# The order of weight and input loads on SyncE's DMA queue in a two-layer attention kernel

## The reference, cut to what matters

```python
def layer(x, emb, mask, ...):                 # H = 16 heads in layer 0, 8 in layer 1
    xn = layernorm(x) * norm_scale + norm_bias
    q, k, v = xn @ Wq + bq, xn @ Wk + bk, xn @ Wv + bv
    # masked rows are left out of the softmax of k over the rows, and of v
    q = softmax(q, within a head)
    k = softmax(k, over the 128 rows)
    attn = einsum('bhsd,bhse->bhde', k, v)
    y = einsum('bhtd,bhde->bhte', q, attn)
    scale, shift = split(silu(emb) @ film_W + film_b)
    h = layernorm(y) * film_norm_scale + film_norm_bias
    h = h * (1 + scale) + shift
    return x + silu(h) @ Wo + bo
out = layer1(layer0(x))
```

## Time and profile before

| | us |
|---|---|
| median of 3 runs | 878.68 |
| the profiled execution | 877.97 |
| its span, first to last instruction | 876.2 |
| TensorE busy | 843.5 (96%) |
| VectorE busy | 679.9 (78%) |
| ScalarE busy | 607.6 (69%) |
| GpSimd busy | 549.5 (63%) |

### The profile page before, as it was taken

How to read it: one execution, slowest core, us unless ns; L and a number is a source line. 1 busy time by engine, 2 the same in 40 slices (tenths; PEclk the granted TensorE clock), 3 DMA queues, 4 the chain that set the end, 5 groups by cost and what they waited for, 6 DMA issues and landing times.

```text
span 876.2 us, 19904 instructions
## 1 busy us (share of the span) xinstructions
PE 843.5 (96%) x6581; PEld 715.2 (82%) x6581; DVE 679.9 (78%) x1352; ACT 607.6 (69%) x1441; POOL 549.5 (63%) x741
## 2 busy tenths in 40 slices
PE   4989999999999999999978999999999999999997
PEld 4768888888888888888867888888888888888885
DVE  5987777778778778877977887787788788777765
ACT  5566777676777677677775866776776777677564
POOL 2475765765766766676657667667656766765541
PEclk9999999999999999999999999999999999999999
DMA  9875766776766665556754656556666655656431
GB/s 315 292 205 172 221 206 188 223 213 196 222 199 204 205 216 186 167 176 192 211 175 151 217 174 200 183 182 196 186 193 199 200 177 178 195 192 198 150 134 61
DMA packets 115549, 169.81 MB, mean 194 GB/s; under 512 B 11871, under 2 KB 84695, under 8 KB 115447
## 3 DMA queue, kind: packets, MB, share of 16 engines
q1 hardware_dynamic: 114656, 167.56, 60.9%
q10 hardware_dynamic: 790, 0.98, 0.4%
HBM read 95.61 MB, written 72.88 MB: 192 GB/s over the span
## 4 chain that ended last, share of the span: by engine, by line
PE 84%; DMA 6%; DVE 4%; issue 2%; ACT 2%; SPq 2%; POOL 0%; ACTq 0%; DVEq 0%
PE PS L1091 74%; PE PS L1187 6%; PE PS L1171 3%; DMA QT<-qy_turned 1%; DMA x_turned<-XS 1%; DMA X<-in_x 1%; DMA qy_turned<-QS 1%; SPq L405 1%; DMA k_turned<-KT 0%; PE PS L1233 0%; SPq L420 0%; DVE WL_k L313 0%; DMA EK<-k_turned 0%; DMA XT<-x_turned 0%; SPq L380 0%
## 5 line engine op out<-in xcount | busy, mean ns | idle before, releaser
L635 POOL TENSOR_TENSOR HL<-H,HH 128x512 fp32r<-128x512 f32 x60 | 78.3, 1305 | 186.6 <-ACT HH L855 186.4
L822 ACT ACTIVATE Z<-QT,FC,FA 128x128 f32<-128x128 f32 x240 | 99.1, 484 | 100.4 <-DMA QT<-qy_turned 100.4
L1091 PE MATMUL PS<-XH,WH_k 128*128 128x256 f32 x512 | 152.0, 297 | 2.6 <-DVE XL L1448 2.5
L1091 PE MATMUL PS<-XH,WL_k 128*128 128x256 f32 x512 | 146.5, 286 | 0.0
L1091 PE MATMUL PS<-XL,WH_k 128*128 128x256 f32 x512 | 146.5, 286 | 0.0
L1091 PE MATMUL PS<-WH_o,HH 128*128 128x512 f32 x248 | 104.2, 420 | 6.6 <-issue 6.4
L892 ACT ACTIVATE XN<-X,NBX,RSX 128x512 f32<-128x512 f32 x60 | 48.8, 813 | 79.2 <-POOL NBX L584 79.2
L1091 PEld LDWEIGHTS PS<-XH,WH_k 128*128 128x128 f32 x512 | 99.9, 195 | 4.2 <-issue 4.1
L784 ACT ACTIVATE SK<-SK,KN 128x128 f32<-128x128 f32 x256 | 98.9, 387 | 5.9 <-DVE KN L1466 5.9
L1091 PE MATMUL PS<-WH_q,XH 128*128 128x512 f32 x256 | 101.4, 396 | 0.3 <-DVE SQ L1493 0.3
L1091 PE MATMUL PS<-WH_v,XH 128*128 128x512 f32 x256 | 100.6, 393 | 0.0
(11 more groups left out here) (155 smaller groups left out, 2111.4 us busy)
## 6 DMA issues: line engine op xcount, KB each, us to landing
qy_turned<-QS SPq DMA_DIRECT2D x60, 512.0 KB, 2.9
QT<-qy_turned SPq DMA_DIRECT2D x240, 128.0 KB, 3.0
k_turned<-KT SPq DMA_DIRECT2D x32, 512.0 KB, 4.1
EK<-k_turned SPq DMA_DIRECT2D x128, 128.0 KB, 2.8
x_turned<-XS SPq DMA_DIRECT2D x30, 512.0 KB, 2.8
XT<-x_turned SPq DMA_DIRECT2D x120, 128.0 KB, 3.5
out_x<-X SPq DMA_DIRECT2D x32, 256.0 KB, 3.4
X<-in_x SPq DMA_DIRECT2D x11, 512.0 KB, 4.9
```

Of the source, the lines that this page charges most:

```text
L635: eng.tensor_tensor(hl_of(o), h_of(o), hh_of(o).bitcast(F32), ALU.subtract).then_inc(pool_hl, 1)
L822: z = eng.activation(z_of(o)[:, c * P:c * P + P].rearrange("p (q n) -> p q n", q=Q), src, ACT.Identity, bias=FC[l][:, c, b:b + 1], scale=F ...
L1091: mm = eng.matmul(dst, left[a](c), right[b](c), start=(c == 0 and a + b == 0), stop=(c == C - 1 and a == 1))
```

## The change

Three edits, all in the order of loads. First, tiles 12 to 15 of x are loaded by one DMA, where there were two, and the load of tiles 16 and 17 goes ahead of the loop; each later load of x is issued four steps sooner, the last one in step 18 where it was step 22. Second, the film loads move from between `write_qy(s)` and `read_qy(s)` of steps 6, 8, ..., 20 to the end of steps 5, 7, ..., 19. Third, the four chunks of K's layer-1 weights move from the same place in steps 22 and 24 to the ends of steps 21 and 22, with one wait for `pe_film` where there were two. `store` and `load_x` change places, which has no effect, since no step issues both.

```diff
-        XLOADS = [(0, 1), (1, 1), (2, 2), (4, 4), (8, 4)] + [(n, 2) for n in range(12, B, 2)]
+        XLOADS = [(0, 1), (1, 1), (2, 2), (4, 4), (8, 4), (12, 4)] + [(n, 2) for n in range(16, B, 2)]
@@ def step(s), SyncE
                 write_qy(s)
-                for n in range(2, 6):
-                    for h in range(2):
-                        if s == FILM_SLOTS[n] - 3 + 2 * h:
-                            load_film(n, h)
-                if s in (22, 24):
-                    eng.wait_ge(pe_film, 6)
-                    load_second(eng, 4, [s - 22, s - 21])
                 for g in x_pair_at(s):
                     read_x(g)
                 read_qy(s)
...
                 masks_at(s)
-                if s < 24 and s % 2 == 0:
-                    load_x(3 + s // 2)
                 if s >= B + 6 and s % 2 == 0:
                     store(s - B - 6)
                     store(s - B - 5)
+                if s < 20 and s % 2 == 0:
+                    load_x(4 + s // 2)
+                for n in range(2, 6):
+                    for h in range(2):
+                        if s == FILM_SLOTS[n] - 4 + 2 * h:
+                            load_film(n, h)
+                if s == FILM_SLOTS[-1]:
+                    eng.wait_ge(pe_film, 6)
+                if FILM_SLOTS[-1] <= s < FILM_SLOTS[-1] + 2:
+                    h = s - FILM_SLOTS[-1]
+                    load_second(eng, 4, [2 * h, 2 * h + 1])
@@ ahead of the loop
             load_x(5)
             eng.wait_ge(pe_film, 2)
             wait_split(3)
+            load_x(6)
             for s in range(5, B - 1):
                 step(s)
```

## The result

The changed kernel takes 886.60 us (median of 7 runs, 883.52 to 889.75) against 879.64 for the kernel before in 7 runs beside it: ratio 1.0078, 95% interval 1.0053 to 1.0102. It is slower by about 7 us, 0.8%. The prediction said 879.2, no change, and a range up to 881.3.

A forecast was written before the change was run, and what follows sets the result against it. TensorE was taken as the bound, idle 1.74 us in the two edited stretches. Terms +0.4, +0.2, +0.3, -0.25, -0.1 sum to +0.55 us on 877.97, giving 878.5; with 0.71 to the median, 879.2, range 877.0 to 881.3.

The forecast's parts named there:

- TensorE bounds the two stretches: From 80.29 to 132.49 and on to 416.93 us, TensorE is busy except 1.74 us, the most a DMA reorder returns.
- The film loads, step 6: Film data ahead of write_qy(6) make read_qy(6) up to 1.9 us late, 0.8 over the margin; +0.4 taken, middle of 0 and 0.8.
- The margin of 1.1: Lateness of QT, read back by read_qy, that output absorbs: less than 1.1 us costs nothing, worked out on QT(6).
- The faster issue of read_qy(8): Without film ahead, its four issues take about 1.7 us instead of 2.6; up to 0.8 us comes back.
- The film loads, the other steps: Steps 8, 16, 20, beside long TensorE steps, and 10, 14, 18 counted at nothing; the margin hides them.
- the small term of step 12: Short gap ahead of write_qy(12), beside a long TensorE step; only lateness through exp_q felt: +0.2 us out of 0 to 0.8.
- goes round the loop: Late QT delays output through film, HH and HL at once, and a later step's read_qy through exp_q.
- its own signs: Trace checks; a difference behind 416.93 us, or holes over 0.5 us in steps 9 to 30, would show it wrong.
- Rival B: Film data at odd steps' ends delay the next write_qy, deciding when over 1.1 us late: +1.9 us, 880.6; chance 0.13.
- The x loads: 1536 KB queued at 79.40 us delay write_x(4), read_x(4) and read_qy(5), the last by up to 1.3 us; +0.3 taken.
- The holes that may go: TensorE idle: step 5's 0.88 us untouched, half of step 8's 0.54 goes (-0.25), second stretch's 0.14 goes (-0.1).
- The likely outcome of no change: Whole kernel within about 0.2%, 1.8 us, of before; chance 0.64.

The follow-up runs named there:

- e9: Kernel before with only half 0 of each film block moved to the ends of steps 5, 9, 13, 17: 879.35 us against 878.42, ratio 1.0008.
- e10: Kernel before with only half 1 of each film block moved to the ends of steps 7, 11, 15, 19: 878.68 us, ratio 0.9999.
- e1: Kernel before with the eight film loads alone moved to the ends of the odd steps: 885.62 us against 880.43, ratio 1.0062.
- e7: Changed kernel with the eight film loads issued on ScalarE's queue in its even step: 888.59 us against 879.15 for the kernel before, ratio 1.0118.
- e2: Kernel before with the x loads alone as in the change: 880.86 us against 880.43, ratio 1.0005.
- e3: Changed kernel with film loads earlier in the same odd steps, between write_keys and place_keys: 881.20 us against 880.43 for the kernel before, ratio 1.0005.
- e5: Changed kernel with each film load of the loop cut to 256 KB: 879.12 us against 879.15 for the kernel before, ratio 1.0003.

## Why the prediction was wrong

- *TensorE bounds the two stretches, and only idle time there can change*: right. All but 0.5 us of the loss there is idle time of TensorE (0.14 to 4.36 in steps 9 to 30). 0.50 of it stands in front of attention(), which waits for EK, a place that the prediction did not have.
- *The film loads, step 6*: the mechanism was right and the size taken wrong. The upper end said 1.9 us late; 2.3 were measured (5.61 for 3.33), and the hole in step 7 is 1.14, not 0.4. The margin of 1.1 was right: 2.3 less 1.1 is nearly the hole. The upper end was built of landings in the trace; its middle with nothing was no estimate. The faster issue of read_qy(8) did not come: it takes 3.03 us now, for 2.56.
- *The film loads, the other steps*: this is the step that failed. Steps 10, 14 and 18 were counted at nothing with the words that the margin hides them. For 8, 16 and 20 the prediction had a reason, the long steps of TensorE behind them, and it held, as it did for the small term of step 12. For 10, 14 and 18 it had none of its own; what set them apart was the pause ahead of their write_qy, 2.5 to 2.8 us in the kernel before against 0.7 to 1.7 in the others. That pause is no constant. It exists because the odd step before is on time, and the load ahead of the even step before that can make it late. e9 and e10 show it: in those steps half 0 alone is covered by the pause, half 1 alone by TensorE's long steps, and half 1 takes half 0's cover away. The hole behind step 10 is 1.02 (pause 1.72), the one behind step 18, the largest, 1.64 (pause 0.71). Step 14 kept a pause of 2.39 and has 0.20 behind it, so how much of the pause goes differs from step to step. The prediction said that what is late "goes round the loop", and then worked out each step from the pauses of the kernel before. By its own signs it is wrong: it allowed no hole over 0.5 us in steps 9 to 30.
- *Rival B* has the right place and the right deciding point, a write over 1.1 us late, with a chance of 0.13 and a price of 1.9; the film loads cost 5.2 (e1). It too took the short-gap steps 6, 8, 12 and 16 for the victims, where 6, 10 and 18 were. By the rule that it cites from the Trainium skill ("DMA: Bandwidth & Descriptors", section "Queues, rings and completion order"), the film delays the write in full. The trace after agrees where the pause is short: 5.2 to 6.1 us in steps 6, 12, 16, 18 and 20, for 2.9. But e7 shows the same delay with the film on another queue, which an order within one queue doesn't give. The prediction let the rule count for little because one row agreed by 0.5 us alone (3.4 for 2.9); in that row only the tail of EK stood ahead.
- *The x loads*, +0.3: nothing that e2 can tell. read_x(4) does go out 1.2 us later in TensorE's step 5 (8.39 for 7.21 us behind its start), where the upper end had 2.1, but read_qy(5) is on time (10.25 for 10.21). *load_second* and the waits for pe_film: nothing, as said; TensorE idles 0.2 us from 309.96 to 423.92, and e3, which has both edits, loses nothing.
- *The holes that may go*: 0.88 in step 5 stayed (0.87), as said. The 0.54 of step 8 fell to 0.17, read_qy(7) being issued 3.5 us after its write in place of 4.6. It was worth 0.4 us, against the 5 lost. In e3 and e5 read_qy(7) again comes 4.5 and 4.6 us after its write, so that slow write can recur.
- *The likely outcome of no change* rested on that margin in every step at once: right in size, but it hides one lateness of under 1.1 us, and the changed kernel's were 2.3 in step 6 and 3.1 in step 18 (write_qy to read_qy 6.08 for 2.94).

## What to carry to other kernels

Put a bulk load on a shared queue where the queue's owner waits for a transfer of its own anyway (behind a write, ahead of the read that waits for it), not at the end of a step when it then stands directly ahead of the next step's first write, as here. When loads are moved into pauses, work out the step after a late one as well: a pause that comes from being on time can't cover two things. And where a lateness goes round a loop, moving half of the loads is a different experiment from moving all, and may cost nothing.

## What the runs showed of the hardware

The start of the kernel differs from execution to execution, whatever the edit: in the twelve profiles TensorE starts step 5 between 79.1 us (e5) and 83.2 us (e1). So does the clock in it. The stretch 64 to 72 us in the kernel before, in the changed one, in e2, and in e1:

```profile
64.00:72.00 8.00, 8.00 (x44) 7.46 (x44) 6.23 (x15) 2.44 (x5) 5.93 (x10) 0.79 0.82 228
```

```profile
64.00:72.00 8.00, 7.27 (x34) 7.22 (x35) 4.79 (x12) 2.31 (x4) 6.82 (x10) 0.57 0.85 253
```

```profile
64.00:72.00 8.00, 8.00 (x38) 7.78 (x39) 4.80 (x11) 2.46 (x5) 6.16 (x10) 0.59 0.80 237
```

```profile
64.00:72.00 8.00, 8.00 (x47) 7.11 (x47) 6.36 (x13) 2.38 (x4) 5.30 (x8) 1.00 0.78 229
```

The granted clock is 0.79, 0.57, 0.59 and 1.00 over the same 8 us; in the 4 us ahead of them TensorE was busy for 1.43, 2.15, 1.42 and 1.43 us. It does not settle the 1.5 us before step 5 by which the changed kernel's profile is behind: e2 had nearly the same clock as the changed kernel there and starts step 5 at 80.7, only 0.4 us behind the kernel before, and e1 with the full clock starts it last. Runs of the kernel before alone spread from 877.18 to 882.79 in 23; what makes the start long or short stays open.

The 2.0 us behind 512 us are idle time of TensorE: 7.45 us (371.45 less 364.00) against 5.53 (369.50 less 363.97). The largest new holes stand in front of output, 1.35 at 522.70 and 0.48 at 792.6. e3, which is not slower than the kernel before, has two like them, 1.18 and 0.35, so they need not be a cost of the new order; where they come from stays open.
